# A fused graph and expert network: all four product buffers of a query group summed by TensorE, six weight products ahead of the loop

## The reference

```python
hg = jnp.einsum('bnf,gf->bng', h3, Wg[:, :F])
qg = jnp.einsum('blf,gf->blg', q, Wg[:, F:]) + bg
attn = jax.nn.sigmoid(hg[:, :, None, :] + qg[:, None, :, :])
qi = jnp.einsum('bnlf,blf->bnf', attn, q)
alpha = jax.nn.sigmoid(jnp.einsum('bnf,gf->bng', h3, Wq[:, :F])
                       + jnp.einsum('bnf,gf->bng', qi, Wq[:, F:]) + bq)
hn = alpha * jnp.tanh(qi) + (1.0 - alpha) * h3
```

## Time and profile before

| | |
|---|---|
| median of 3 runs | 1924.17 us (1922.68 to 1926.90) |
| profiled execution | 1920.13 us, its span 1918.0 us |
| TensorE busy | 1730.7 us, 90% of the span |
| VectorE busy | 708.6 us, 37% |
| ScalarE busy | 438.5 us, 23% |
| GpSimd busy | 177.0 us, 9% |
| first query loop | from 166.5 us |
| second query loop | from 433.5 us |

### The profile page before, as it was taken

The page is one execution under the profiler, slowest core; times in us unless marked ns, Lnnn a source line. Parts: engine busy times, 40 slices in busy tenths (PEclk is TensorE's granted clock), DMA queues, the critical chain, the costliest instruction groups (busy, mean ns, idle before and its releaser), DMA issues.

```text
span 1918.0 us, 26881 instructions
## 1 busy us (share of the span) xinstructions
PE 1730.7 (90%) x11856; PEld 1043.3 (54%) x11856; DVE 708.6 (37%) x1179; ACT 438.5 (23%) x816; POOL 177.0 (9%) x81
## 2 busy tenths in 40 slices
PE   7997867997767999999999998887999899999999
PEld 4674433573435655567764443333566555766666
DVE  4325998008997222154321000001423232234220
ACT  0014555115663111043311000000521010131110
POOL 0002443004441000000000000000002000000000
PEclk9999899999999999989989999999999999999999
DMA  9216653617544677730358999999734336212650
GB/s 376 99 45 210 149 142 122 246 46 197 143 156 163 237 309 297 284 144 6 143 197 356 418 428 429 428 428 429 300 149 168 114 135 261 83 66 108 264 223 18
DMA packets 80748, 408.25 MB, mean 213 GB/s; under 512 B 9768, under 2 KB 50240, under 8 KB 58992
## 3 DMA queue, kind: packets, MB, share of 16 engines
q1 hardware_dynamic: 76112, 402.41, 55.0%
q10 hardware_dynamic: 4512, 4.03, 0.7%
HBM read 400.85 MB, written 5.51 MB: 212 GB/s over the span
## 4 chain that ended last, share of the span: by engine, by line
PE 69%; DVE 13%; DMA 12%; issue 4%; ACT 2%; POOL 0%; SPq 0%; DVEq 0%; ACTq 0%
PE banks L114 67%; DVE weight_ring L120 10%; DMA weight_ring<-in_L_ffn_c_fc_dram 7%; PE banks L117 2%; DMA weight_ring<-in_L_gnn_W_in_dram 2%; DMA weight_ring<-in_L_ffn_c_proj_e_dram 1%; ACT weight_ring L148 1%; DVE stat L266 1%; DMA gate_queries<-in_L_gnn_query_rep_dram 1%; DVE xn_tok L125 0%; DMA node_parts<-gate_node_parts 0%; DMA ident<-in_c_ident_dram 0%; DVE xT L137 0%; DVE stat L268 0%; DVE rgat_xr L137 0%
## 5 line engine op out<-in xcount | busy, mean ns | idle before, releaser
L120 DVE TENSOR_TENSOR weight_ring<-weight_ring,gate_queries 128x1024 f32<-128x1024 f32 x192 | 308.2, 1675 | 17.4 <-ACT weight_ring L148 16.2
L114 PE MATMUL banks<-weight_ring,xT 128*128 128x384 f32 x864 | 292.3, 490 | 2.4 <-DVE rgat_xr L137 1.5
L114 PEld LDWEIGHTS banks<-weight_ring,xT 128*128 128x128 f32 x864 | 161.9, 191 | 109.6 <-issue 9.0
L148 ACT ACTIVATE weight_ring<-banks 128x1024 f32<-128x1024 f32 x192 | 185.5, 1026 | 134.5 <-PE banks L114 134.4
L120 POOL TENSOR_TENSOR weight_ring<-weight_ring 128x1024 f32<-128x1024 f32 x46 | 150.3, 3266 | 429.2 <-DVE weight_ring L120 429.2
L114 PE MATMUL banks<-xT,weight_ring 128*128 128x256 f32 x792 | 182.2, 385 | 3.2 <-ACT x_tok L151 3.2
L114 PEld LDWEIGHTS banks<-xT,weight_ring 128*128 128x128 f32 x792 | 153.3, 194 | 31.2 <-issue 7.3
L114 PE MATMUL banks<-weight_ring,selrow 128*32 128x256 f32 x1168 | 81.5, 413 | 79.3 <-DVE weight_ring L120 79.1
L114 PE MATMUL banks<-weight_ring,r_xd 128*32 128x384 f32 (+1 forms) x2304 | 142.7, 406 | 1.1 <-DVE r_xd L124 0.6
L114 PE MATMUL banks<-weight_ring,moe_xdT 128*64 128x384 f32 x720 | 122.0, 489 | 21.7 <-DMA weight_ring<-in_L_ffn_c_fc_dram 20.7
L114 PE MATMUL banks<-gate_rows,selrow 96*128 96x512 bf16 x384 | 112.5, 406 | 12.0 <-ACT weight_ring L148 6.8
(11 more groups left out here) (371 smaller groups left out, 1856.3 us busy)
## 6 DMA issues: line engine op xcount, KB each, us to landing
weight_ring<-in_L_ffn_c_fc_dram SPq DMA_DIRECT2D x30, 2304.0 KB, 23.8
weight_ring<-in_L_ffn_c_proj_e_dram SPq DMA_DIRECT2D x21, 2304.0 KB, 28.3
gate_queries<-in_L_gnn_query_rep_dram SPq DMA_DIRECT2D x48, 512.0 KB, 4.0
weight_slot_heads<-in_L_ffn_c_proj_e_dram SPq DMA_DIRECT2D x9, 2304.0 KB, 28.3
weight_ring<-in_L_ffn_w_gate_dram SPq DMA_DIRECT2D x8, 2304.0 KB, 9.4
weight_ring<-in_L_ffn_w_up_dram SPq DMA_DIRECT2D x8, 2304.0 KB, 9.1
weight_ring<-in_L_ffn_w_down_dram SPq DMA_DIRECT2D x8, 2304.0 KB, 9.2
weight_ring<-in_L_ffn_w_dram SPq DMA_DIRECT2D x16, 1152.0 KB, 8.2
```

Of the source, the lines that this page charges most:

```text
L114: return self.e.matmul(out, lhsT, rhs, start=start, stop=stop)
L120: return self.e.tensor_tensor(out, a, b, op)
L148: return self.e.activation(out, a, f, **kw)
```

## The change

- `gate_pool` is gone, and with it the 46 additions and the wait for `folded`. TensorE sums all four buffers of each group.
- The first six weight products stand ahead of the loop, before the wait for the matrix `Wqi`, and in the first layer behind one for the query terms' split (their bank was in use). The rest is spread as 13/6 a group where it was 5/2, and the two left over come behind the last sums.
- The last 12 products go pair by pair of output chunks: for each pair the two of chunk 4 and the two of chunk 5, then its mark.
- In the first layer SyncE issues the query rows of groups 0 to 2 ahead of the last write of query parts and the last four row reads, not behind them.

```diff
--- before.py
+++ after.py
@@ -800,11 +800,15 @@
             q.turns.append((counts.slot["work", l], ("Wqi", l)))
             if l == 0:
                 for b in range(QB):
+                    if b == QB - 2:
+                        for G in range(RBUF):
+                            queries_sp(q, l, G)
                     if b % 2 == 0:
                         query_parts_sp(q, b // 2)
                     query_rows_sp(q, 0, b)
-            for G in range(RBUF):
-                queries_sp(q, l, G)
+            else:
+                for G in range(RBUF):
+                    queries_sp(q, l, G)
             for b in range(QB):
                 q.wait_ge(*(at(f"gate_rows_{b % 2}", (l, b - 2, "nodes") if b >= 2 else (l, QB - 2 + b, "queries"))))
                 if b == QB // TC:
@@ -909,6 +913,10 @@
 
             pe.wait_ge(*at("kept", "gate_sel"))
             pe.wait_ge(*loaded(("Wqh", l)))
+            if l == 0:
+                pe.wait_ge(*at("split_rest", (NQ - 1, "biased")))
+            for i in range(DC):
+                beside(i)
             pe.wait_ge(*loaded(("Wqi", l)))
             for n in range(STEPS):
                 G, t = divmod(n, NQL)
@@ -917,7 +925,7 @@
                     pe.wait_ge(*at(f"gate_rows_{b % 2}", (l, G, "nodes")))
                 fill_pe(pe, l, n)
                 if t == 0:
-                    for i in range((5 * G + 1) // 2, (5 * G + 6) // 2):
+                    for i in range(DC + 13 * G // 6, DC + 13 * (G + 1) // 6):
                         beside(i)
                 elif t == 1 and b == 1 and j:
                     pe.wait_ge(*at("qi_act", (l, "sb", j - 1)))
@@ -927,26 +935,27 @@
                 elif t == 2 and G:
                     if b == 1 and j:
                         pe.wait_ge(*at("qi_act", (l, "T", j - 1)))
-                    pe.wait_ge(*at("folded", (l, G - 1)))
                     pe.wait_ge(*at("weighed", (l, NQL * G - 1)))
-                    for u in (0, 2, 3):
+                    for u in range(NQL):
                         m = query_sum_pe(pe, l, G - 1, u)
                     m.then_inc(*mark("qi_ps", (l, G - 1)))
             for u in range(NQL):
                 pe.wait_ge(*at("weighed", (l, STEPS - NQL + u)))
                 m = query_sum_pe(pe, l, GROUPS - 1, u)
             m.then_inc(*mark("qi_ps", (l, GROUPS - 1)))
+            for i in range(DC + 13 * GROUPS // 6, (DC - 2 + DC) * DC):
+                beside(i)
             pe.wait_ge(*at("qi_act", (l, "sb", NREL - 1)))
             for f in range(2):
                 turn_qi_pe(pe, f, 2 * f, 0).then_inc(*mark("qi_ps", (l, "turned", NREL - 1 + f)))
             pe.wait_ge(*at("qi_act", (l, "T", NREL - 1)))
-            for o in range(DC):
-                query_product(o, DC - 2)
-            pe.wait_ge(*at("qi_dve", (l, "T")))
-            for o in range(DC):
-                t = query_product(o, DC - 1)
-                if o % 2:
-                    t.then_inc(*(mark("node_ps", (l, o // 2)) if o < DC - 1 else mark("unit_free", ("Wqi", l))))
+            for g in range(DC // 2):
+                for f in (DC - 2, DC - 1):
+                    if f == DC - 1:
+                        pe.wait_ge(*at("qi_dve", (l, "T")))
+                    for o in (2 * g, 2 * g + 1):
+                        t = query_product(o, f)
+                t.then_inc(*(mark("node_ps", (l, g)) if g < DC // 2 - 1 else mark("unit_free", ("Wqi", l))))
 
         def gate_act(a, l):
             for c in range(TC):
@@ -1028,13 +1037,6 @@
                 v.then(v.tt(gth[:, o2, :], gth[:, o2, :], galpha[:, o2, :], ALU.mult))
                 v.tt(hT[:, o2, :], hT[:, o2, :], gth[:, o2, :], ALU.add).then_inc(*mark("gated", (l, g)))
 
-        def gate_pool(g, l):
-            for G in range(GROUPS - 1):
-                w = [products(l, NQL * G + t) for t in range(2)]
-                g.wait_ge(*at("weighed", (l, NQL * G + 1)))
-                g.tt(w[0], w[0], w[1], ALU.add).then_inc(*mark("folded", (l, G)))
-
-
         def L0_gnn_sp(q):
             start_sp(q)
             gate_sp(q, 0)
@@ -1072,8 +1074,6 @@
 
         def L0_gnn_pool(g):
             norm_pool(g, "L0_gnn")
-            for l in range(2):
-                gate_pool(g, l)
 
         def L0_gnn_dve(v):
             start_dve(v)
```

## The result

| | median us | lowest to highest | runs |
|---|---|---|---|
| kernel before | 1923.6 | 1922.68 to 1926.9 | 4 |
| changed kernel | 1865.28 | 1862.57 to 1871.87 | 4 |

The ratio is 0.9699, with a 95% interval of 0.9671 to 0.9727: some 58 us less. Forecast were 1858.5 us, in a range of 1838 to 1884. The profiled execution of the changed kernel took 1871.87 us (span 1869.8), 48.3 less than the profiled execution of before, and 6.6 above its own median. The steps that the forecast names gave 61.3 us, near its 65.6; some 13 were lost in places that it doesn't name.

What follows compares the result with a forecast made beforehand. VectorE's multiplications, stretched by GpSimd's additions, were taken to bound the query loops. Loop 0 -35.6 and loop 1 -30.0, together -65.6 from 1920.13, give 1854.5; with 4.0 for the median 1858.5 us, range 1838 to 1884.

Steps and rivals of the forecast that it cites:

- the price of the addition: Query loops: GpSimd's addition costs VectorE 2.17 us a group, 100 us in all, by stretching one multiplication.
- The period: Settled group of the query loops: falls from 6.70 to 4.93 us, bounds 4.53 and 5.4.
- The two rings: Query loops: sums-fill-sigmoid-multiplication closes at 4.93 us, TensorE's own order at 4.94; both agree on the group's length.
- the second ring: TensorE's own order: sums, last fill, two sigmoids, third fill, then 0.43 to the next sums; 4.94 us.
- The seams: Groups 8/9 and 16/17: ScalarE's copies make a group 6.39 us, 1.46 more each, 2.9 per loop.
- The stalls: Fourth group of each loop: VectorE waits 6 us for late query rows, bounds 3 and 9; slower clock adds 2.
- The start: Ahead of loop 0: reordered query rows let the loop start 1.5 us earlier, bounds -4 and +1.
- The mark behind the loops: Last products pair by pair: next projections start 1.1 us earlier behind loop 0, 0.2 behind loop 1.
- All later weight loads hang on the loops' ends, and shift with them: Behind the loops: later weight loads move with the loops' ends; no further term given.
- The VectorE-bound case: Rival, query loops: VectorE stays the bound at 4.53 us a group, no stalls; about 1825 us, chance 0.08.
- Transfers: Rival, query loops: transfers or clock set the group's length at 5.6 us; about 1889 us, chance 0.10.
- Slower: Rival, query loops: TensorE's lower clock makes the kernel slower, 1930 to about 2011 us, chance 0.02.

Runs made afterwards that it cites:

- dead_addition: Changed kernel, four sums on TensorE, plus a GpSimd addition into a scratch tile that nobody reads: 1923.1 us, ratio to before 1.0012.
- keep_addition: Changed kernel with GpSimd's addition put back and three sums on TensorE, everything else kept: 1920.2 us, ratio to before 0.9983.
- sum_each_step: Changed kernel with TensorE's sums spread, one buffer's behind each fill instead of four together behind one fill: 1874.4 us, ratio to before 0.9735.
- loads_in_parts: Changed kernel with the fourth group's query rows issued ahead of the 2.3 MB weight load, and that load in six parts: 1854.0 us, ratio to before 0.9619.
- old_query_order: Changed kernel with the three query-row transfers issued in the order of the kernel before: 1870.8 us, ratio to before 0.9712.

## Why the prediction was right, and where not

| step | forecast us | measured us |
|---|---|---|
| start of loop 0 | -1.5 | -0.6 |
| loop 0 with stall and clock | -33.0 | -31.1 |
| behind loop 0 | -1.1 | -0.9 |
| start of loop 1 | +1.6 | +1.4 |
| loop 1 with stall and clock | -31.4 | -30.0 |
| behind loop 1 | -0.2 | -0.1 |
| sum of these | -65.6 | -61.3 |
| ahead of the projection | 0 | +2.6 |
| behind both loops | 0 | +10.5 |

- **What bounds, and the price of the addition: right.** dead_addition and keep_addition show that the stretching of one multiplication in a group is the whole effect, at 2.16 us each, against 2.17 read from the trace of before. The reason given for it, a multiplication begun before the addition that still runs beside its first microsecond, is right too. It was taken as an objection to full blocking; it is full blocking, with GpSimd as the one that waits first. One reading was too strong: the chain passes TensorE and ScalarE as well in the first loop up to 228 us (the earlier trace rows show ScalarE at 193.75), and VectorE alone only from there to 311.
- **The period: right ring, one term too small.** The two rings at 4.93 and 4.94 were the right ones to see; VectorE alone (4.53) would have been 10% off. The term that was too small, by 0.10 us, is "then 0.43 for it" in the second ring: the last fill to the next sums takes 0.53. Over 46 periods this is 5.1 us. The same changes between kinds of products raise TensorE's work in a group from the forecast's 4.3 to 4.59 us, which did no harm here but made the obvious next step, sum_each_step, a loss.
- **The seams: right**, 1.34 more each against 1.46.
- **The stalls: right in place and size.** 6.39 and 5.88 us against 6 each, and with the half-speed group behind them 7.9 and 7.3 against 8. loads_in_parts took away 15.3 us, and these waits were what it removed. In loop 0 landing and need both came later than forecast (191.3 for 187.6, 184.9 for 181.3), nearly all of it because the loop itself began at 168.5 and not at 165.0, so their difference held.
- **The start: too hopeful by 0.9 us.** The step was "the write of node parts then leaves about 0.5 us later". It left 4.7 us later by the clock of the profile (162.24 against 157.54; some 2.6 of that is the later start of the whole stretch), since it waits on its queue for reads that wait for the query parts' write, itself slowed from 3.3 to 6.1 us. That it nevertheless pays is shown by old_query_order: 21.2 us in place of 19.2.
- **The mark behind the loops: right**, -0.9 and -0.1.
- **"All later weight loads hang on the loops' ends, and shift with them": this is the step that failed.** The later work shifted by 58.7 us as far as the first expert layer's end, and then lost 10.5. 9.6 of these went at the pause at 778.38 with the clock behind it. A change of TensorE's instruction count moves everything behind it in the instruction stream, too, and I gave this no term. The 2.6 us ahead of the projection lie in unchanged code: the first multiplication starts between 168.1 and 172.6 us in the kernels of this study, with no order by edit.
- **The rivals.** The VectorE-bound case fell (0.41 us of idle time in each group), though without the stalls and with pairs of sums the kernel comes to 1840.3, a good part of the way to its 1825. Transfers didn't set the period (no wait for one in a settled group at a share of 0.72), and in the loops the clock fell behind the stalls (0.50 in 195 to 200 us). "Slower" fell: TensorE's granted clock is 1.00, 2.4 GHz, in the whole of 224 to 286.

The forecast of 1858.5 us lies 6.8 below the median, and that it is so near is in part luck. Against the profiled execution, from which all steps were read, the forecast was 1854.5 and the measurement 1871.87 us: 17.4 more, 4.3 in the named steps and 13.1 outside them. The profiled execution of before lay 4.0 us below its median, that of the changed kernel lies 6.6 above its own, and this closes most of the gap. What the 6.6 are can't be told from one profile.

## What to carry to other kernels

Before taking work off a waiting chain, look at what an engine does to its neighbour: a "helping" GpSimd operation that nobody waited for cost the bound engine 2.16 us each time, about the 2.21 that it took once its turn had come. Read such a price from starts and ends, not from the helper's recorded length, which here held about 1 us of its own waiting. When such a bound falls, work out every ring that closes within a few tenths of it, count the changes between kinds of products on TensorE as work, and look for the transfer that was late all along. And where a loop's instruction count changes, expect unchanged code behind it to change by some microseconds; compare equal instructions of the two traces before giving such a difference to the edit.

## What the runs showed that I had not expected

- A GpSimd addition and VectorE's multiplications, all reading SBUF tiles, take turns completely: the addition ends 2.20 to 2.22 us behind the multiplication that it met, and the next multiplication 1.08 to 1.09 behind the addition, in 136 groups of three kernels.
- A change on TensorE from the fills (bf16, 512 columns wide, 96 rows) to the sums (float32, on 32 of the array's columns) costs 0.10 us, and back 0.14 us (0.53 and 0.57 from start to start, where 0.43 is the work). Eight changes in a group and not two move the period from 5.04 to 5.29 us, four and earlier sums to 4.81.
- TensorE can stand 6.0 to 6.6 us shortly behind a conditional branch, waiting for nothing that the profile shows; with what follows the eight kernels lose 6.9 to 10.0 us there, the changed kernel 9.6. Sixteen tiny products at the program's start, some 770 us ahead of it, make it go.
- A 512 KB transfer issued behind a 2.3 MB one on the same queue landed after 11.1 and 11.2 us (the median of the 48 is 4.0). At the moment when the loop has the least buffered, this cost 15.3 us in two loops.
